# The stores of a Mamba-style layer move from SyncE's DMA queue to GpSimd's

## What is computed

```python
xn = _layernorm(x)
x = x + attn_ref(xn, ...) + ffn_ref(xn, ...)

# attn_ref (a selective scan; D_MODEL 1024, D_INNER 2048, D_STATE 16, DT_RANK 64)
x = _rmsnorm(resid, norm_w)
skip = x @ skip_w.T
x = silu(_causal_depthwise_conv(x @ in_w.T, conv_w, conv_b))
delta = softplus(x @ wd1.T @ wd2.T + wd2_b)
Bm, Cm = x @ wb.T, x @ wc.T
y = _selective_scan(x, delta, Bm, Cm, A)    # h = exp(dt*A)*h + dt*x*B ; y = sum_n h*C
y = (y + x * W_D) * silu(skip)
return resid + y @ out_w.T

# ffn_ref: gate/up/down of 2816, both operands of each product quantized to FP4 in blocks of 16
```

## Time and profile before

| | us |
|---|---|
| two timed runs | 10489.23 and 10498.07, median 10493.65 |
| the profiled execution, its own time | 10475.34 |
| its span, from the first to the last instruction, on the slowest core | 10473.8 |
| spans of the 8 cores | 10452.7 to 10473.8 |
| VectorE busy | 6135.3 (59%) |
| TensorE busy | 2915.8 (28%) |
| ScalarE busy | 2230.7 (21%) |
| GpSimd busy | 823.6 (8%) |

### The profile page before, as it was taken

How to read it: one execution, slowest core, us unless ns; L and a number is a source line. 1 busy time by engine, 2 the same in 40 slices (tenths; PEclk the granted TensorE clock), 3 DMA queues, 4 the chain that set the end, 5 groups by cost and what they waited for, 6 DMA issues and landing times.

```text
span 10473.8 us, 50658 instructions; the slowest of 8 cores (10452.7 to 10473.8 us)
## 1 busy us (share of the span) xinstructions
PE 2915.8 (28%) x8880; PEld 965.9 (9%) x8880; DVE 6135.3 (59%) x5976; ACT 2230.7 (21%) x2910; POOL 823.6 (8%) x312
## 2 busy tenths in 40 slices
PE   1111125545441333311111113444322222222224
PEld 0000011211110000000000001111000000000001
DVE  5666654434431222289999982222299997999940
ACT  1222211111113111123333320111122222222200
POOL 0000000000000000034444440000000000000000
PEclk9999996666665555555555556666555555555557
DMA  1111210010010110010000002111201112111122
GB/s 49 44 47 43 62 59 13 10 47 30 31 35 28 51 37 36 36 62 19 16 24 16 16 20 77 45 44 44 85 36 48 40 45 82 54 64 62 54 66 74
DMA packets 214754, 460.18 MB, mean 44 GB/s; under 512 B 114416, under 2 KB 115056, under 8 KB 191216
## 3 DMA queue, kind: packets, MB, share of 16 engines
q1 hardware_dynamic: 206960, 422.33, 11.7%
q0 software_dynamic: 7488, 34.61, 1.0%
HBM read 296.71 MB, written 160.17 MB: 44 GB/s over the span
## 4 chain that ended last, share of the span: by engine, by line
DVE 57%; PE 14%; DMA 10%; ACT 9%; issue 8%; DVEq 1%; ACTq 1%; SPq 0%; POOLq 0%
DVE s3o_hb L54 11%; DVE pf_ub L54 7%; DVE pf_E L54 6%; DVE s3o_ub L54 5%; DVE s3o_hcb L54 3%; PE c3o_pssk L825 2%; PE c3p_psx L759 2%; DVE c3p_cb L54 2%; DVE c3o_cb L54 2%; DVE q_t L54 2%; DMA sdelta<-c3o_db 1%; DMA sdelta<-c3p_db 1%; DVE p2q_t L54 1%; PE c_pso L1262 1%; PE c3o_psx L759 1%
## 5 line engine op out<-in xcount | busy, mean ns | idle before, releaser
L54 DVE TENSOR_TENSOR_SCAN s3o_hb<-s3o_ab,h_sb,s3o_ub 128x2048 bf16<-128x2048 f32 x256 | 1147.8, 4484 | 83.4 <-ACT s3o_ab L103 58.1
L54 POOL TENSOR_TENSOR pf_ub<-pf_dxt,pf_Brep 128x1536 f32<-128x1536 f32 x256 | 795.7, 3108 | 4074.9 <-DVE pf_c L54 3104.5
L103 ACT ACTIVATE s3o_ab<-s3o_dt,A_sb 128x2048 f32<-128x2048 f32 x256 | 512.5, 2002 | 1427.3 <-DVE s3o_hb L54 1414.5
L54 DVE TENSOR_TENSOR pf_ub<-pf_dxt,pf_Brep 128x512 f32<-128x512 f32 x256 | 780.7, 3050 | 26.7
L103 ACT ACTIVATE pf_E<-pf_c,pf_bias,nA_sb 128x2048 f32<-128x2048 f32 x256 | 535.9, 2093 | 980.9 <-DVE pf_E L54 962.7
L1013 PE MATMUL s3o_psht<-eye_sb 128*128 128x128 bf16 x768 | 203.7, 265 | 1862.3 <-DVE s3o_hb L54 1163.4
L1195 PE MATMUL pf_psht<-eye_sb 128*128 128x128 bf16 x768 | 202.0, 265 | 1596.1 <-DVE pf_ub L54 1026.7
L54 DVE SCALAR_TENSOR_TENSOR pf_E<-pf_E,pf_ub 128x2048 f32<-128x2048 f32 x256 | 608.5, 2377 | 26.7
L54 DVE TENSOR_TENSOR s3o_ub<-s3o_dxt,s3o_Brep 128x2048 f32<-128x2048 f32 x256 | 586.8, 2292 | 27.0 <-DVE s3o_hcb L54 0.5
L103 ACT ACT_TABLE_LOAD x180 | 230.9, 1283 | 1455.7 <-PE p_psu L584 320.2
L54 DVE TENSOR_TENSOR p_h<-p_h,p_psu 128x512 f32<-128x512 f32 (+1 forms) x96 | 61.8, 643 | 753.3 <-ACT p_h L103 753.3
(11 more groups left out here) (164 smaller groups left out, 5996.6 us busy)
## 6 DMA issues: line engine op xcount, KB each, us to landing
s3o_dt<-sdelta SPq DMA_DIRECT2D x32, 1024.0 KB, 5.9
s3o_xct<-sxc SPq DMA_DIRECT2D x32, 1024.0 KB, 4.8
sxc<-c3p_xc SPq DMA_DIRECT2D x64, 256.0 KB, 2.3
sdelta<-c3p_db SPq DMA_DIRECT2D x64, 256.0 KB, 2.4
pf_dt<-sdelta SPq DMA_DIRECT2D x16, 1024.0 KB, 4.8
pf_xct<-sxc SPq DMA_DIRECT2D x16, 1024.0 KB, 4.8
sxc<-c3o_xc SPq DMA_DIRECT2D x64, 256.0 KB, 2.4
sskip<-c3o_skb SPq DMA_DIRECT2D x64, 256.0 KB, 2.5
```

Source lines behind the costliest of these rows:

```text
L54: instr = attr(*a, **k)
L103: scalar.activation(out=out, in_=in_, func=func, **kw).then_inc(kb.sems["S"], 1)
```

## The change

Every store of the two chunk stages and of the own scan is issued by GpSimd instead of SyncE and counted on Stg instead of St: `sxc`, `sskip`, `sB`, `sC`, `sdelta`, `sypart` and `sym`. The waits that protect the stored buffers name Stg accordingly. ScalarE's copy to `dlowb` gets a wait for Stg where it had none. The loads that read these tensors back wait for Stg too: `Brep` in both scans and `ymt` in the output projection. The loads of `in_w`, `skip_w` and `out_w` go on waiting for St alone. At the very end SyncE also waits for Stg and Lg. Loads, arithmetic and buffers stay as they are.

```diff
                     sba.wait("V", v_cv)
-                    sba.wait("St")
+                    sba.wait("Stg")
                     s_xc = sba.act(xcb[:], cb2[:], AF.Silu, bias=convb_sb[:, et:et + 1])
...
-                    @B.sync
-                    def _(sync):
-                        kb.wait(sync, "S", s_xc)
-                        kb.dma(sync, sxc[et * 128:(et + 1) * 128, c0:c0 + CH], xcb[:], sem="St")
+                    @B.gpsimd
+                    def _(gpsimd):
+                        kb.wait(gpsimd, "S", s_xc)
+                        kb.dma(gpsimd, sxc[et * 128:(et + 1) * 128, c0:c0 + CH], xcb[:], sem="Stg")
...
                 sba.wait("Tn", t_dl)
+                sba.wait("Stg")
                 sba.act(dlowb[:], ps_dl[:], AF.Copy)
                 sba.act(bcb[:, 0:CH], ps_B[:], AF.Copy)
                 s_dl = sba.act(bcb[:, CH:2 * CH], ps_C[:], AF.Copy)
...
-                @B.sync
-                def _(sync):
-                    kb.wait(sync, "S", s_dl)
-                    kb.dma(sync, sB[:, c0:c0 + CH], bcb[:, 0:CH], sem="St")
-                    kb.dma(sync, sC[:, c0:c0 + CH], bcb[:, CH:2 * CH], sem="St")
+                @B.gpsimd
+                def _(gpsimd):
+                    kb.wait(gpsimd, "S", s_dl)
+                    kb.dma(gpsimd, sB[:, c0:c0 + CH], bcb[:, 0:CH], sem="Stg")
+                    kb.dma(gpsimd, sC[:, c0:c0 + CH], bcb[:, CH:2 * CH], sem="Stg")
...
                     sba.wait("V", v_zb2)
-                    sba.wait("St")
+                    sba.wait("Stg")
                     sba.act(db[:], zb[:], AF.Exp)
                     s_db = sba.act(db[:], db[:], AF.Ln, bias=1.0)
...
-                    @B.sync
-                    def _(sync):
-                        kb.wait(sync, "S", s_db)
-                        kb.dma(sync, sdelta[et * 128:(et + 1) * 128, c0:c0 + CH], db[:], sem="St")
+                    @B.gpsimd
+                    def _(gpsimd):
+                        kb.wait(gpsimd, "S", s_db)
+                        kb.dma(gpsimd, sdelta[et * 128:(et + 1) * 128, c0:c0 + CH], db[:], sem="Stg")
...
                     kb.wait(sync, "St")
+                    kb.wait(sync, "Stg")
                     kb.wait(sync, "Tn")
                     kb.wait(sync, "Sg")
                     kb.dma(sync, Brep[:], sB[nh * 8:(nh + 1) * 8, :].partition_broadcast(128))
```

More of the change, by code:

```diff
@@ L832, in p3_chunks @@
                         sba.wait("Tn", t_bc)
-                        sba.wait("St")
+                        sba.wait("Stg")
                         s_sk = sba.act(skb[:], ps_sk[:], AF.Silu)
-                        @B.sync
-                        def _(sync):
-                            kb.wait(sync, "S", s_sk)
-                            kb.dma(sync, sskip[et * 128:(et + 1) * 128, c0:c0 + CH], skb[:], sem="St")
+                        @B.gpsimd
+                        def _(gpsimd):
+                            kb.wait(gpsimd, "S", s_sk)
+                            kb.dma(gpsimd, sskip[et * 128:(et + 1) * 128, c0:c0 + CH], skb[:], sem="Stg")
                 t_dl = kb.cnt["Tn"]
@@ L1034, in p3_scan, with _ @@
                             sba.flush(B)
[L1036 to L1039, removed]
+                            @B.gpsimd
+                            def _(gpsimd):
+                                kb.wait(gpsimd, "S", s_y)
+                                kb.dma(gpsimd, sypart[et * 128:(et + 1) * 128, :], ytl[:], sem="Stg")
                         else:
@@ L1047, in _ @@
                                 kb.wait(vector, "L", ld_sk)
-                                kb.wait(vector, "St")
+                                kb.wait(vector, "Stg")
                                 for sg in range(4):
@@ L1057, in p3_scan, with _ @@
                             v_ym = kb.cnt["V"]
[L1059 to L1062, removed]
+                            @B.gpsimd
+                            def _(gpsimd):
+                                kb.wait(gpsimd, "V", v_ym)
+                                kb.dma(gpsimd, sym[et * 128:(et + 1) * 128, :], ymb[:], sem="Stg")
                     sba.flush(B)
@@ L1286, in _ @@
         kb.wait(sync, "St")
+        kb.wait(sync, "Stg")
+        kb.wait(sync, "Lg")
         if dbg is not None:
```

## The result

The changed kernel took 10608.07 us in the median of 7 runs (10597.53 to 10616.86); the kernel before, measured beside it, 10490.54 us in the median of 6 (10478.78 to 10503.38). The ratio is 1.011 with a 95% interval from 1.0098 to 1.0122: 1.1% slower, 117.5 us (103 to 128 by the interval), where 109.4 had been forecast.

The account below looks back on a forecast made before the run. The chunk stretches were taken as chains of waits for store landings. Terms 81.6 + 10.9 + 13.8 + 3.9 + 2.0 - 2.8 = 109.4 us (147x + 9.4), on 10493.65, gave 10603 us, 1.0% slower; range 10533 to 10700.

Parts of the forecast that it names:

- The bound: Both chunk stretches: chains of short waiting steps; 120 sdelta stores that ScalarE waits for, 81.6 us more.
- x = 0.68: Every store whose landing is waited for: 0.68 us more from GpSimd, 0.48 before the record plus 0.2 to landing.
- sB and sC: Chunk stages: sC waits for sB and each chunk's first Exp for both; 8 x 2 x 0.68 = 10.9 us more.
- The new wait before dlowb: ScalarE before dlowb: 13.8 us more in the own chunks, waiting for skb's store, and 3.9 in the prefix chunks.
- xc, skb and the scan at nothing: 192 xc and skb stores with 3.5 us to spare and 32 scan stores: no cost.
- The loads of Brep: Three loads of Brep wait for the last store before them: 3 x 0.68 = 2.0 us more.
- The outwT loads: First load of outwT no longer waits for the last sym store and goes earlier: -2.8 us.
- The sum at x = 0.4: Estimate from the skill's first-byte times, GpSimd about 1 us, SP about 0.6: the whole sum below 68 us.
- VectorE holding the store back through zb: Rival at the sdelta store: descriptors wait for zb, 0.99 us per store, 155 us in all, 10649 us; chance 0.14.
- A landing longer by 1.35 us: Rival: stores cost as much more as the 1408 KB loads, 1.83 us each, 278 us, 10772 us; chance 0.11.
- a landing sooner than SyncE's: Rival at the same 136 waited-for stores: GpSimd's land sooner after the record, so not slower, 10485 us; chance 0.06.
- Stores that are no links: Rival: something else would have ended the waits for the stores; sum 10 to 20 us, 10510 us; chance 0.03.

Follow-up runs that it names:

- k1: The changed kernel with the 128 sdelta stores back on SyncE and St: 10518.17 us, ratio 1.0029 to the kernel before.
- k4: The kernel before with only the sdelta stores moved to GpSimd and Stg, Brep loads waiting for Stg too: 10582.59 us, ratio 1.0091.
- k2: The changed kernel without ScalarE's new wait before the copy to dlowb: 10591.36 us, ratio 1.0101 to the kernel before.
- k9: The kernel before with only the xc, skb, sypart and sym stores on GpSimd, no wait before dlowb: 10483.73 us, ratio 1.000.
- k10: The changed kernel with SyncE in the own scan waiting for GpSimd's store to land before prefetching dt and xct: 10603.87 us, ratio 1.0113.
- k3: The changed kernel with two zb buffers, so VectorE computes zb before the sdelta store: 10603.29 us, ratio 1.0111 to the kernel before.
- k7: The changed kernel with an unused float32 copy on VectorE before each zb, beside the sdelta store: 10655.66 us, ratio 1.0163.
- k6: The changed kernel with four db buffers, a store semaphore each, and two zb buffers: 10217.73 us, ratio 0.9747 to the kernel before.

## Why the prediction was right

- **The bound.** The chunk stretches were read as chains of waits, and the tile view named the 120 stores. k1 and k4 give 90 and 96.5 us for them and the waits themselves 89.8, forecast 81.6. Nearly the whole miss of 8 us lies in this term.
- **x = 0.68.** Measured 0.75: the 0.48 before the record is 0.47, and the 0.2 of landing, taken from 512 KB loads, is 0.3 for 256 KB stores. The load was a good stand-in; the 1408 KB load and SyncE's 16 KB store, the ends of the range, were far off.
- **sB and sC.** ScalarE's wait for sC grew by 9.4 us in the prefix chunks and 2.3 in the own ones, 11.7 against 10.9 forecast. Two single events are in this and partly cancel: one odd gap (below) adds 3.2 us to the 9.4, and one sB store of the own chunks before, which landed after 3.5 us where the median was 1.6, takes some 1.9 off the other. Without both it would be 10.4.
- **The new wait before dlowb.** 3.3 us in the row shown, forecast 3.4. With the prefix chunks' share 17.7 us were forecast; k2 gives 16.7 by the times of the kernels and 15.9 by the two stages.
- **xc, skb and the scan at nothing.** k9: 1.000 +- 0.001. For the scan it was the cover that was right and not the landing: sypart's store took 4.0 us longer to land and not 0.7, and an et of 73 us hid that too.
- **The loads of Brep.** The forecast has 3 x 0.68 = 2.0 us. From the end of the last Ln (or of the last copy to ytl) to the issue of Brep, the shortest case among the eight cores grew from 2.60, 2.66 and 4.18 us to 3.36, 3.42 and 4.94, by 0.76 each, 2.3 in all.
- **The clock at nothing.** TensorE's granted clock was 0.59 in the prefix chunks before and after, and 0.62 and 0.61 in the own ones.
- **The outwT loads.** The first was to go 2.8 us earlier. It is issued 0.29 us after ymb's end at 10175.20, before 2.90 us after it: 2.6. The end of the kernel did not become shorter for it in the profiled pair, 433.2 us from ymb's start against 424.5. Over the eight cores it took 424.5 to 431.2 us before and 427.8 to 440.4 after, and in k10, which has the same end, 426.5 to 435.8. Whatever the 2.6 us give is hidden in this scatter; the term of -2.8 us is not shown.
- **The sum at x = 0.4.** It is 147 x 0.4 + 9.4 = 68.2 us, just above the 68 that the prediction puts it below. The 117.5 us measured are far from it, and the 0.47 us before the record alone are more than 0.4.
- **Rivals.** VectorE holding the store back through zb: refuted by k3. The argument that was put against it, a record that started inside a VectorE operation in the earlier trace rows, carries little: that operation was a reduction, and in k7 the record started inside the copy as well and was held all the same, which showed in its length and not in its start. A landing longer by 1.35 us, and a landing sooner than SyncE's: both refuted by the 2.6 and 2.7 us. Stores that are no links: refuted by k1.

## What to carry to other kernels

A store's queue matters only where somebody waits for the landing: read in the tile view whose idle time a DMA ends, count the cases, and multiply by the difference from the end of the producer to the landing, the dispatch before the record included, since that was the larger part here. Where the list is long, more buffers, each with a semaphore of its own, are worth far more than the choice of queue: four db buffers and two zb gave 283 us here, against 117 lost by the queue. Two zb alone (k3) left the time at 10603.29 us, within the scatter of the changed kernel's 10608.07. And when a wait is added "to be safe", look for whether an earlier wait already covers it.

## What the runs showed of the hardware that was not expected

- A float32 copy on VectorE, SBUF to SBUF, stretched GpSimd's DMA record from 0.54 to 0.92 us and the landing by 0.4 us, the record ending with the copy (k7). The operation zb, which reads PSUM, did nothing of the kind (k3).
- A 1024 KB store of GpSimd with 1024 KB loads of SyncE beside it, one after the other, landed after 8.7 us, alone after 4.1; on SyncE's queue, issued 0.6 us ahead of the same loads, it took 4.7. The store started 0.4 us after the first load's issue in the changed kernel, and came off worse than the load, whose landing in the median was 6.6 us against 4.8 in k10. No run tells the part of the queue from that of the order of issue.
- In the changed kernel one sC store, in the fourth prefix chunk, was issued 5.1 us after sB, where the others took some 2.2:

```profile
4424.37 0.51 POOL L130 DMA_DIRECT2D sB<-c3p_bcb  x1 [6.09 <-ACT c3p_bcb L103]
4429.47 0.50 POOL L130 DMA_DIRECT2D sC<-c3p_bcb  x1 [4.59 <-issue]
```

The profile names nothing that GpSimd waited for. It is no chance event, and not the only one. Counted among GpSimd's DMAs, this store is the 172nd, and its record starts 3.42 us after the landing that it waits for, where the seven other sC stores of the profiled core have 0.53. The 3.42 us stand on all eight cores of the changed kernel and of k2, k3, k7 and k10. On all of these cores, too, the 117th (an sdelta store) comes 1.9 us after its Ln, where 0.6 is usual, and the 289th (xc) and the 405th (sym) 3.4 us after their producers. In k6 the 172nd comes late as well, after 2.95 us. k4 and k9 have no store in common, and yet in both it is the 114th and the 166th DMA whose record comes after 1.9 and 3.35 us:

```profile
4475.23 0.55 POOL L130 DMA_DIRECT2D sdelta<-c3p_db  x1 [5.53 <-issue]
...
4339.38 0.55 POOL L130 DMA_DIRECT2D sxc<-c3p_xc  x1 [12.11 <-issue]
```

The first row is the 114th DMA of k4, the second that of k9. The delay goes with the place in GpSimd's own stream of instructions, not with the store or its stage. It costs 1.3 and 3.2 us at the first two places of the changed kernel, where the store is a link, and nothing seen at the others. What causes it was not tried and stays open.
